# Decoder megakernel, mLSTM stage: two heads' score products side by side in two 64-row halves of TensorE, four score banks, one output bank

## The reference, cut to what matters

```python
ig, fg  = x_k_v @ Wi + bi, x_k_v @ Wf + bf         # one input and one forget gate for each head and token
log_D   = tril(cumsum(log_sigmoid(fg))_s - cumsum(...)_t) + ig_t
D       = exp(log_D - max_t log_D)
C       = (q_h @ k_h.T) / sqrt(16) * D             # scores of one head, 256 x 256, weighted and masked
Cn      = C / (max(|sum_t C|, exp(-max log_D)) + 1e-6)
h       = Cn @ v_h ; h = layernorm_over_16(h) * ln_scale
x       = layernorm(x + h)
```

## Time and profile before

| | |
|---|---|
| device time, median of 3 runs | 1911.98 us (1905.87 to 1913.06) |
| the profiled execution | 1905.86 us, its span 1904.0 us |
| TensorE, VectorE, ScalarE, GpSimd busy | 83%, 69%, 55%, 32% of the span |
| loop of this stage over its 64 units | about 1724 to 1815 us of the span |
| mean granted TensorE clock | 0.874 of 2.4 GHz |

### The profile page before, as it was taken

How to read it: one execution, slowest core, us unless ns; L and a number is a source line. 1 busy time by engine, 2 the same in 40 slices (tenths; PEclk the granted TensorE clock), 3 DMA queues, 4 the chain that set the end, 5 groups by cost and what they waited for, 6 DMA issues and landing times. The chain is left out here.

```text
span 1904.0 us, 26882 instructions
## 1 busy us (share of the span) xinstructions
PE 1578.8 (83%) x8949; PEld 960.7 (50%) x8949; DVE 1306.5 (69%) x2697; ACT 1045.6 (55%) x2072; POOL 604.5 (32%) x543
## 2 busy tenths in 40 slices
PE   6967899999999788899979789774999877548935
PEld 3753466666677553556563356652223334227722
DVE  3766867677666443888668469438999766864668
ACT  2113555556554324798747658325999732625635
POOL 0404543131300000898525030013990000435620
PEclk9979999999999989899999879887555588778969
DMA  5100000000000100111026240016999900020000
GB/s 218 29 1 28 1 1 1 1 1 1 1 1 1 47 17 24 45 45 55 13 50 112 60 89 2 26 72 161 183 184 185 158 23 6 1 88 1 1 1 23
DMA packets 213689, 93.07 MB, mean 49 GB/s; under 512 B 205968, under 2 KB 206992, under 8 KB 211888
## 3 DMA queue, kind: packets, MB, share of 16 engines
q1 hardware_dynamic: 213408, 90.97, 21.0%
q10 hardware_dynamic: 144, 0.39, 0.1%
HBM read 39.36 MB, written 1.11 MB: 21 GB/s over the span
## 5 line engine op out<-in xcount | busy, mean ns | idle before, releaser
L1078 POOL TENSOR_TENSOR ss_u<-dx,b_rows 128x512 f32<-128x512 f32 x128 | 158.9, 1274 | 241.0 <-POOLq L186 224.3
L773 ACT ACTIVATE gq_p<-gq_s,gq_bias,gq_rq 128x512 f32<-128x512 f32 x128 | 98.5, 773 | 119.0 <-DVE gq_bias L843 119.0
L1160 DVE TENSOR_TENSOR_SCAN ss_h<-ss_decay,ss_u 128x512 f32<-128x512 f32 x128 | 146.4, 1204 | 24.9 <-PE ss_ht L1118 19.2
L2136 ACT ACTIVATE qc_p<-qc_s,qc_bias,sq 128x1024 int16<-128x1024 f32 x128 | 154.2, 1204 | 16.3 <-DVE qc_bias L2102 6.2
L706 POOL TENSOR_TENSOR gq_xw<-gq_x,weights 128x512 f32<-128x512 f32 x48 | 67.8, 1413 | 294.4 <-ACT gq_x L733 293.7
L2100 DVE TENSOR_REDUCE qc_mx<-qc_s 128x1 f32<-128x1024 f32 x128 | 155.4, 1214 | 4.7 <-PE qc_s L2035 4.7
L2035 PE MATMUL qc_s<-kT,qT 64*128 64x512 bf16 x256 | 130.8, 618 | 15.0 <-ACT qc_p L2136 7.3
L1132 PE MATMUL ss_acc<-ss_hc,consts 128*128 128x512 f32 x256 | 131.4, 597 | 0.0
L641 PE MATMUL gq_s<-gq_KT,gq_QT 128*128 128x512 f32 x256 | 122.0, 600 | 3.6 <-ACT gq_p L773 3.6
L663 PE MATMUL gq_o<-gq_pT,gq_V 128*128 128x256 f32 x512 | 121.2, 379 | 1.4 <-DVE gq_pT L877 1.4
L840 DVE TENSOR_REDUCE gq_mx<-gq_s 128x1 f32<-128x512 f32 x128 | 88.2, 691 | 44.0 <-PE gq_s L641 43.6
(11 more groups left out here) (615 smaller groups left out, 3827.0 us busy)
## 6 DMA issues: line engine op xcount, KB each, us to landing
b_rows<-b_rows SPq DMA_DIRECT2D x16, 512.0 KB, 3.5
weights<-in_weights SPq DMA_DIRECT2D x1, 6152.0 KB, 18.3
weights<-in_weights SPq DMA_DIRECT2D x1, 5248.0 KB, 16.7
weights<-in_weights SPq DMA_DIRECT2D x1, 3072.0 KB, 9.8
weights<-in_weights SPq DMA_DIRECT2D x2, 1155.0 KB, 5.0
weights<-in_weights SPq DMA_DIRECT2D x1, 2156.0 KB, 7.4
qc_pT<-qc_p SPq DMA_TRANSPOSE x128, 3.4
weights<-in_weights SPq DMA_DIRECT2D x1, 1410.0 KB, 9.1
```

Source lines behind the costliest of these rows:

```text
L773: nc.scalar.activation(pr[c % 2][:, t, :], sc[t][:, :], ACT.Exp, bias=bias[:, c, t:t + 1], scale=rq[b % 2][:, t, u:u + 1], accum_out=sm[:, ...
L1078: nc.gpsimd.tensor_tensor(u_in[i % 3][:, :], dx[:, m, hf * HT:hf * HT + HT], rows.rows[c % 2][:, n % rows.NEACH, :], ALU.mult).then_inc(in ...
L1160: nc.vector.tensor_tensor_scan(h[group % 2][:, m, :], decay[i % 2][:].rearrange("p b t -> p (b t)"), u_in[i % 3][:, :], 0.0, ALU.mult, ALU ...
L2136: nc.scalar.activation(pi[i % R][:, :], sc[i % 3][:, :], ACT.Exp, bias=bias[:, i:i + 1], scale=sq[:, t, h:h + 1], accum_out=sm[:, i:i + 1] ...
```

## The change

Each masked product now takes 64 rows in place of 128. A half of 128 channels is cut into an upper and a lower 64 rows with four heads each; the constant `fourth` keeps head m of each 64 rows, so four GpSimd operations for each sequence mask what eight did. The scores of a pair of heads, one in rows 0 to 63 and one in rows 64 to 127, are made by products that stand next to each other in the order, into two different banks. Score banks become four, two for each pair in turn; the eight banks allow only one output bank `po` then, so each `outputs` waits for the copy of the group before. The masks are split off from `scores` (their own semaphore `masked`), and the order on TensorE becomes masks, scores of a pair, masks. The heads run in the order 0, 4, 2, 6, 1, 5, 3, 7 of each half, and indices of outputs follow. The gates' transposes use two of the score banks, and the second pair waits until these are read. A constant `paired` is added and not used.

```diff
+        fourth=(p // 16 % 4 == np.arange(4)[None, :]).astype(f),
...
-        sc = [pb(f"mc_s{i}", [P, 512]) for i in range(3)]
+        sc = [pb(f"mc_s{i}", [P, 512]) for i in range(4)]
-        po = [pb(f"mc_o{i}", [P, S]) for i in range(2)]
+        po = pb("mc_o", [P, S])
-        qm = [g.gap[:, 0:4096].rearrange("p (j c s) -> p j c s", j=8, c=2), sb("mc_qm", [P, 8, 2, S])]
+        qm = [g.gap[:, 0:2048].rearrange("p (m c s) -> p m c s", m=4, c=2), sb("mc_qm", [P, 4, 2, S])]
...
                 def mask_queries(b):
                     if b >= 2:
-                        pool.wait_ge(scored, 16 * (b - 1))
-                    for j in range(8):
-                        nc.gpsimd.tensor_scalar(qm[b % 2][:, j], g.XT[:, :, b * S:b * S + S], g.eighth[:, j:j + 1], 0.25,
+                        pool.wait_ge(scored, 8 * (b - 1))
+                    for m in (0, 2, 1, 3):
+                        nc.gpsimd.tensor_scalar(qm[b % 2][:, m], g.XT[:, :, b * S:b * S + S], g.fourth[:, m:m + 1], 0.25,
                                                 ALU.mult, ALU.mult).then_inc(q_masked, 1)
...
-            def scores(u):
-                b, hd = u // 16, u % 16
-                if u >= 3:
-                    nc.tensor.wait_ge(weighted, u - 2)
-                if hd < 8:
-                    nc.tensor.wait_ge(q_masked, 8 * b + hd + 1)
-                c, t0 = hd // 8, b * S
-                s, qh = sc[u % 3], qm[b % 2][:, hd % 8, c, :]
-                nc.tensor.matmul(s[:, 0:S], g.CT[:, c, t0:t0 + P], qh, start=True, stop=True)
-                nc.tensor.matmul(s[:, S:S + P], g.CT[:, c, t0 + P:t0 + S], qh[:, P:S], start=True, stop=True)
+            def head(u):
+                return u % 16 // 8 * 8 + u % 8 // 4 + (0, 4, 2, 6)[u % 4]
+
+            def scores(p):
+                b, hd = p // 8, head(2 * p)
+                c, m, t0 = hd // 8, hd % 4, b * S
+                nc.tensor.wait_ge(q_masked, 4 * b + (1, 3, 2, 4)[m])
+                if p == 1:
+                    nc.tensor.wait_ge(at_made, 2)
+                    nc.tensor.wait_ge(floored, 2)
+                if p >= 2:
+                    nc.tensor.wait_ge(weighted, 2 * p - 2)
+                for keys, cols, first in ((t0, slice(0, S), 0), (t0 + P, slice(S, S + P), P)):
+                    for k in range(2):
+                        e = slice(64 * k, 64 * k + 64)
+                        last = nc.tensor.matmul(sc[2 * (p % 2) + k][:, cols], g.CT[e, c, keys:keys + P],
+                                                qm[b % 2][e, m, c, first:S], start=True, stop=True)
+                last.then_inc(scored, 1)
+
+            def masks(u):
+                t0, hd = u // 16 * S, head(u)
                 if u >= 2:
                     nc.tensor.wait_ge(exped, 2 * (u - 1))
...
             def outputs(i):
...
-                if i >= 2:
-                    nc.tensor.wait_ge(out_stored, i - 1)
+                if i >= 1:
+                    nc.tensor.wait_ge(out_stored, i)
...
-                for i in range(U + 6):
-                    if i < U:
-                        scores(i)
-                    if i >= 2 and (i - 2) % 4 == 3 and i - 2 < U:
-                        outputs((i - 2) // 4)
-                    if i >= 4 and (i - 4) % 4 == 3 and i - 4 < U:
-                        out_turns((i - 4) // 4)
+                for p in range(U // 2 + 2):
+                    if p < U // 2:
+                        masks(2 * p)
+                        scores(p)
+                        masks(2 * p + 1)
+                    if p >= 2 and p % 2 == 0:
+                        outputs(p // 2 - 1)
+                    if p >= 3 and p % 2 == 1:
+                        out_turns((p - 3) // 2)
...
                 def exponents(u):
-                    b, hd = u // 16, u % 16
-                    act.wait_ge(scored, u + 1)
+                    b, hd = u // 16, head(u)
+                    act.wait_ge(masked, u + 1)
...
-                    if u >= 3 and (u - 3) % 4 == 3 and u - 3 < U:
-                        store_out((u - 3) // 4)
+                    if u >= 5 and u % 4 == 1:
+                        store_out((u - 5) // 4)
...
+                        dve.wait_ge(scored, u // 2 + 1)
                         dve.wait_ge(exped, 2 * u + 2)
```

More of the change, by code:

```diff
@@ L133, in shape_constants @@
         eighth=(p // 16 == np.arange(8)[None, :]).astype(f),
+        paired=(p // 16 == np.array([0, 2, 4, 6, 1, 3, 5, 7])[None, :]).astype(f),
+        fourth=(p // 16 % 4 == np.arange(4)[None, :]).astype(f),
         inv_freq=rows(inv_freq), ones=np.ones((P, P), f),
@@ L2689, in L3_xattn @@
                 block, ctx_in, gates, gstored, forgets, f_made, a_made, m_made, fm_made, parts_made, chain, turned, at_made, floored,
-                zeroed, ones_made, v_made, q_masked, ahead_sum, ahead_total, compared, made, scored, exped,
+                zeroed, ones_made, v_made, q_masked, ahead_sum, ahead_total, compared, made, scored, masked, exped,
                 weighted, used, out_stored, out_turned, done, nchain, centred, squared, var_summed,
@@ L2723, in _ @@
                 mask_queries(1)
-                pool.wait_ge(zeroed, 3)
+                pool.wait_ge(zeroed, 2)
                 compare(0, 5)
@@ L2752, in scores @@
                 nc.tensor.matmul(m[:, S:S + P], sel, parts[:, t0 + P:t0 + S], start=True, stop=False)
-                nc.tensor.matmul(m[:, S:S + P], g.ident_b, g.deny_kb, start=False, stop=True).then_inc(scored, 1)
+                nc.tensor.matmul(m[:, S:S + P], g.ident_b, g.deny_kb, start=False, stop=True).then_inc(masked, 1)
             def outputs(i):
@@ L2758, in outputs @@
                 if i == 0:
[L2759 removed]
+                    nc.tensor.wait_ge(zeroed, 2)
                 if c == 0:
                     nc.tensor.wait_ge(v_made, 2 * b + 2)
[L2762 to L2763 removed]
+                if i >= 1:
+                    nc.tensor.wait_ge(out_stored, i)
                 for k in range(4):
[L2765 to L2766 removed]
+                    nc.tensor.matmul(po[32 * k:32 * k + 17, :], v[:, 2 * b, c // 2 * 8 + c % 2 + 2 * k, :],
+                                     w[(4 * i + (0, 2, 1, 3)[k]) % 8][:, 0:2, :].rearrange("p a b -> p (a b)"), start=True, stop=False)
                 for k in range(4):
[L2768 to L2769 removed]
+                    last = nc.tensor.matmul(po[32 * k:32 * k + 17, P:S], v[:, 2 * b + 1, c // 2 * 8 + c % 2 + 2 * k, :],
+                                            w[(4 * i + (0, 2, 1, 3)[k]) % 8][:, 2, :], start=False, stop=True)
                 last.then_inc(used, 1)
@@ L2792, in turn_gates @@
                     nc.tensor.wait_ge(floored, 1)
-                for ps, src in ((po[0], a), (po[1], fm)):
+                for ps, src in ((sc[2], a), (sc[3], fm)):
                     for t in range(4):
@@ L2856, in store_out @@
                         act.wait_ge(out_turned, i - 1)
-                    nc.scalar.copy(ob[i % 2][:, :], po[i % 2][:, :]).then_inc(out_stored, 1)
+                    nc.scalar.copy(ob[i % 2][:, :], po[:, :]).then_inc(out_stored, 1)
                 def square(b):
@@ L2934, in finish_group @@
                     dve.wait_ge(out_turned, i + 1)
-                    nc.vector.tensor_copy(o[:, 2 * b:2 * b + 2, 4 * c:4 * c + 4, :], pot[:, :, :, 0:17]).then_inc(done, 1)
+                    nc.vector.tensor_copy(o[:, 2 * b:2 * b + 2, c // 2 * 8 + c % 2:c // 2 * 8 + 8:2, :], pot[:, :, :, 0:17]).then_inc(done, 1)
                 def memory_steps(b):
@@ L2985, in _ @@
                 dve.wait_ge(floored, 2)
-                for i in range(2):
-                    nc.vector.memset(po[i][:, :], 0.0).then_inc(zeroed, 1)
+                nc.vector.memset(po[:, :], 0.0).then_inc(zeroed, 1)
                 steps = iter(())
@@ L4149, in program @@
         g.eighth = const("eighth")
+        g.paired, g.fourth = const("paired"), const("fourth")
         g.inv_freq = const("inv_freq")
```

8 lines of the change are left out of this document (4 added, 4 removed).

## The result

Five runs of the changed kernel gave a median of 1893.37 us (1891.71 to 1896.10), five of the kernel before 1907.18 (1905.85 to 1913.06). The ratio is 0.9929, with a 95% interval of 0.9911 to 0.9947. So the change made the kernel 0.7% faster: 13.8 us by the two medians, some 13.5 us by the ratio. The profiled execution took 1895.54 us with a span of 1893.7, where before it was 1905.86 and 1904.0.

What follows compares the result with a forecast made beforehand. TensorE was taken to bound the 90 us loop. A group falls from 5.35 to 4.24 us, 17.7 over 16 groups, less 1 for VectorE and 1 for table changes: 16 us off 1911.98, 1896 us, range 1885 to 1905.

Steps and rivals of the forecast that it cites:

- likeliest case: Whole kernel: 13 to 18 us of gain, 1896 us, own range 1885 to 1900; chance 0.68.
- Two halves at once: Loop's score products: two heads in row halves stream together, 0.76 us a pair in place of 2 x 0.71.
- rival of halves one behind the other: Loop's score products: f32 row halves run in sequence, group 5.66 us, loop 5 us longer, 1917 us; chance 0.06.
- The switches: TensorE in the loop: each change of the array's shape costs 0.09 us, charged on both sides of a pair's scores.
- Outputs and transposes: End of each group: outputs 0.87 us, transposes 0.28 plus 0.05 for a late f32 load, wait for the copy gone.
- The waits in the loop: Loop: slack shrinks as groups shorten; 1 us charged for VectorE and 1 us for ScalarE's table changes.
- Changes of tables: ScalarE, twice in the loop: with less slack TensorE waits some 0.5 us more each, 1 us in all.
- VectorE and ScalarE: Loop: VectorE's work of 4.65 us in heavy groups exceeds the 4.24 us group; 1 us charged in all for VectorE.
- The 28 us behind the loop: Code behind the loop, mostly VectorE's (18.62 us busy): expected to stay as before.
- the change leaves both alone: The 28 us behind the loop and the 30 us of gates ahead: untouched, so only the loop can pay.
- rival of the lower level over the whole loop: TensorE's clock falls to 1.2 GHz: group 7.8 us in place of 5.35, 39 us more, 1951 us; chance 0.04.
- GpSimd: Masking in the loop: 16 operations of 0.69 us in place of 32, beside TensorE's work, worth nothing.

Runs made afterwards that it cites:

- experiment 5: Changed kernel with the square root of the variance replaced by a copy, so ScalarE doesn't change tables in the loop: 1890.66 us, ratio 0.9919 to the kernel before.
- experiment 4: Changed kernel with LayerNorm's square put back ahead of the outputs' copy on ScalarE: 1894.71 us, ratio 0.9935 to the kernel before.
- experiment 2: Changed kernel with both score products of one row half written before the two of the other: 1894.57 us, ratio 0.993 to the kernel before.
- experiment 6: Changed kernel with GpSimd making each masked query twice, the second into an unread spare tile: 1892.15 us, ratio 0.9929 to the kernel before.
- experiment 7: Changed kernel with outputs and transposes one pair later and ScalarE's outputs' copy ahead of that place's exponents: 1889.15 us (0.9911), second run 1890.22 us (0.9916).
- experiment 3: Changed kernel with two masks of a pair's second unit between its 256- and 128-column scores, four switches a pair: 1906.44 us, ratio 0.9993 to the kernel before.

## Why the prediction was right, point by point

**The time.** 1896 forecast, 1893.37 measured, in the likeliest case's own range (1885 to 1900). The gain was forecast as 16 us from 1911.98. That median of the runs then shown was high: with two more it is 1907.18, and the changed kernel is 12.1 to 13.8 us below the kernel before in all three comparisons. So the gain was forecast some 2 to 4 us too large: one of the three comparisons lies within its bounds of 13 to 18, two just below. That 1896 came within 3 us of the result owes something to luck. From 1907.18 the same sum gives 1891, below the result; the high start and the large gain are errors of opposite sign. The forecast for the profiled execution, 1889.9, shows the second alone: it had 1895.54.

**Two halves at once.** Right. A pair's scores with both switches were put at 0.09 + 0.76 + 0.09 = 0.94 and measured 0.09 + 0.86 = 0.95. The rival of halves one behind the other falls: that was 0.76 + 0.71, and no timeline shows it. In the group above the four pairs of passes of the changed kernel start at 1742.924 and 1742.930, 1743.244 and 1743.250, 1743.461 and 1743.468, 1743.569 and 1743.576: two halves at a time, 6 or 7 ns apart.

**The switches.** The 0.09 a switch held, at the change to row halves and at that to column strips. The Trainium skill (TensorEngine Tiling (Array Packing), Key Properties) says that changing the mode drains the engine; read as a full drain that would have been 0.16. The trace shows that there is a price, and a smaller one than by that reading.

**Outputs and transposes.** Outputs 0.87 as forecast (0.78 and the gap ahead). The transposes were put at 0.28 + 0.05 and took 0.22: the late f32 load that I had charged does not stand there. That is the 0.10 between 4.24 and 4.14, 1.6 us over 16 groups, and the quiet group lies just under the 4.2 to 4.4 us of the prediction. TensorE's wait for the outputs' copy is gone, as forecast.

**The waits in the loop.** Right in kind. Between the first and the last outputs stand 15 steps. At 5.35 - 4.14 = 1.21 each that would be 18.15 us, and 15.2 came. The missing 2.9 us can be read off the steps:
- *Changes of tables.* Forecast 0.5 more for each than before. The two steps were 6.71 - 5.34 = 1.37 over a quiet one before, and 1.77 and 1.49 now: 0.4 and 0.1 more, 0.5 in all. Experiment 5 shows that the excess of these two steps comes with the table changes.
- *VectorE and ScalarE.* Forecast 1 us. Three more steps were over 4.14 (4.43, 4.22 and 4.99), by 1.2 us together, where before none was. They are there without the table changes too (4.45, 4.23 and 4.98 in experiment 5). In two of them, the first and the last, the waits name VectorE's copy of the transposed outputs and its weighting, which come late in the part of the loop where LayerNorm's steps lie between them. No experiment took these steps away, so this cause is read from the waits and not shown:

```profile
1771.01 0.62 PE L2778 MATMUL mc_o<-weights,mc_v 128*17 128x256 f32 x8 [0.15 <-DVE weights L3009]
...
1787.97 0.41 PE L2790 MATMUL mc_ot<-consts,mc_ob 128*128 128x128 f32 x2 [0.22 <-DVE mc_o L2950]
...
1790.27 0.63 PE L2778 MATMUL mc_o<-weights,mc_v 128*17 128x256 f32 x8 [0.38 <-DVE weights L3009]
```

- *The last step.* It was 4.46 before, since no new scores stand in its second half, and 4.36 now: it gained 0.1 and not 1.2. Its outputs wait for the last weighting, 0.96 before and 1.03 now. The forecast took 16 full groups and did not see this; the 1.4 us gained ahead of the first outputs make up for it.

**The 28 us behind the loop.** Here the prediction was wrong: it left them alone. They grew by 1.7 us, because the diff also changes ScalarE's order: the copy of the outputs now stands ahead of the square, so the square waits for the last outputs, and VectorE's variance waits 1.31 us for the square. Experiment 4 undid that and took 1.5 of the 1.7 away, though in its profile the loop lost some 0.5 by it. The step that failed is "the change leaves both alone": the diff moved an instruction on ScalarE, and I had looked at what the copy waits for and not at what stands behind it.

**The clock.** The rival of the lower level over the whole loop falls: from 1731 on the loop runs at 1.00. But right behind the first table change, after TensorE had waited 1.29 us, the profiled run of experiment 4 fell to 0.50 for 3.4 us; that group took 7.4 us, where it is 5.9 in the changed kernel without such a fall. The profiles of experiments 2, 6 and 7 show such long groups (7.3 to 7.6 us), the three profiles of the changed kernel don't (5.9). The length of the wait alone does not decide it: in experiment 2 the fall came behind one of 0.98 us, and the changed kernel's three profiles, with 0.97 to 0.99 at the same place, had none. In those of the changed kernel, time was lost elsewhere, in unchanged code behind the stage: the granted clock there was 0.81 to 0.85 in three stretches, where the second run of experiment 7 had it at 1.00 from a like place on. First the changed kernel, then experiment 7:

```profile
1838.70:1843.70 5.00, 3.32 (x19) 1.64 (x16) 3.13 (x6) 3.59 (x6) 0.00 (x0) 0.84 0.00 0
1843.70:1848.70 5.00, 2.47 (x15) 1.16 (x14) 4.69 (x12) 2.92 (x4) 0.00 (x0) 0.85 0.02 3
1848.70:1853.70 5.00, 3.22 (x22) 1.66 (x21) 3.92 (x9) 3.22 (x4) 0.00 (x0) 0.81 0.00 0
```

```profile
1838.40:1843.40 5.00, 3.25 (x8) 1.04 (x8) 4.79 (x10) 2.10 (x4) 0.00 (x0) 0.65 0.00 0
1843.40:1848.40 5.00, 2.60 (x21) 1.40 (x22) 4.76 (x10) 3.85 (x5) 0.00 (x0) 1.00 0.01 3
1848.40:1853.40 5.00, 3.22 (x28) 1.98 (x27) 4.60 (x10) 3.33 (x4) 0.00 (x0) 1.00 0.00 0
```

Over the eleven profiles of kernels with the change or a variant of it the code ahead of the stage, the same in all, ended between 1690.1 and 1696.5 us, and the one behind it was 66.4 to 71.2 us long. So the -2.4 and the -2.0 of the table above lie within what the profiles of these kernels span. But the three profiles of the changed kernel differ among themselves by 1.3 and 0.8 us only, and each has 2.0 to 2.8 us more behind the stage than the one profile of the kernel before. This agrees with the times: from the first gate product to the last transposes the stage gained 14.5 to 15.1 us (143.18 before; 128.47, 128.12 and 128.65), and less the 2.0 to 2.8 behind it this is near the 12.1 to 13.8 of the medians. So the forecast's 16 was 1 to 1.5 us too large for the stage, and the rest was lost in code that it took to be untouched, with a lower granted clock in its rows. What sets where the clock falls was not isolated, and the kernel before has a single profile: this part stays open, and no more than a few us hang on it.

**GpSimd.** Its halved masking is worth nothing, as forecast (experiment 6).

## What to carry to other kernels

Products of 64 rows and f32 in two row halves do run together: two heads took the time of one, and the price was 0.09 us for each change of the array's shape and a late f32 load. So put work of one shape together: two more changes for each pair of heads (experiment 3) took the whole gain away, and one fewer in each group (experiment 7) made a group 0.11 us shorter. And where a diff reorders one engine's list, read what stands behind the moved instruction up to the stage's last one: here the new order cost 1.5 us at the end, and the old one some 0.5 within the loop.

## What the runs showed of the hardware that was not expected

- TensorE's products did not start in program order across row halves: the second half's first product started 14 ns behind the first half's, though three passes of the first half stand between them in the program, the last two of which started 0.54 us later or more (experiment 2). The Trainium skill (TensorE: Matmul & The Clock Gate, Part 3) says that matmuls start and end strictly in order; the starts in this trace do not agree for two row halves (the ends are modelled).
- A change of the array's shape costs more than its gap when f32 products follow: the piece of two halves with 128 columns took 0.42 us from its start to the next masks, and each added pair of changes 0.31 us in a quiet group, of which the two gaps of 0.09 are 0.18 (experiment 3).
- The granted clock fell to 0.50 for 3.4 us in the midst of a full loop, right behind a wait of 1.29 us (experiment 4). It fell behind a wait of 0.98 us in experiment 2 too, and behind waits of 0.97 to 0.99 us at the same place in the three profiles of the changed kernel it did not.
